# A four-block kernel: in the state-space stage the skip term goes to the matmul engine, the triangle to GpSimd, and one product changes its place; in the routing stage a subtraction is made in eight pieces

## The reference

```python
z, xBC, dt = split(x @ W_in)                       # 256, 384, 4 columns
xBC = silu(conv_b + sum(xp[:, k:k + L] * conv_w[:, k] for k in range(4)))
xh, B, C = split(xBC)                              # 4 heads of 64, 64, 64
dt = softplus(dt + dt_bias);  dA = dt * -exp(A_log);  A_cum = cumsum(dA)
Lmat = exp(where(tril, A_cum[l] - A_cum[s], -inf))  # the triangle
Y = einsum('ln,sn,hls,shp->lhp', C, B, Lmat, xh * dt)
Y = (Y + xh * D[:, None]) * silu(z)                # xh * D is the skip term
Y = Y * rsqrt(mean(Y * Y) + eps) * norm_w
out = Y @ W_out @ W_lin + b_lin
```

## Time and profile before

| | before |
|---|---|
| median of 3 runs | 1223.52 us (1223.49 to 1224.08) |
| the profiled execution: its own time | 1222.53 us |
| its span, first to last instruction | 1220.7 us |
| outside the span | 1.8 us |
| PE busy | 1028.3 us (84%) |
| DVE busy | 842.0 us (69%) |
| ACT busy | 712.4 us (58%) |
| POOL busy | 388.8 us (32%) |
| mean granted clock of PE | 0.901 |

### The profile page before, as it was taken

The page is one execution under the profiler, slowest core; times in us unless marked ns, Lnnn a source line. Parts: engine busy times, 40 slices in busy tenths (PEclk is TensorE's granted clock), DMA queues, the critical chain, the costliest instruction groups (busy, mean ns, idle before and its releaser), DMA issues. The chain is left out here.

```text
span 1220.7 us, 23165 instructions
## 1 busy us (share of the span) xinstructions
PE 1028.3 (84%) x6680; PEld 898.8 (74%) x6680; DVE 842.0 (69%) x2130; ACT 712.4 (58%) x1561; POOL 388.8 (32%) x421
## 2 busy tenths in 40 slices
PE   2999999999995857999998875567429999899997
PEld 2988988889884624666666664466419999799997
DVE  4577777877766468999999945799845555345554
ACT  4556565565662468889888825666315555355554
POOL 4223232232330000111111112556743444434445
PEclk9999999999998877888888777788559999899999
DMA  5121211211200023232223206534244444333331
GB/s 160 50 82 44 79 50 43 86 43 49 71 0 23 20 69 66 58 69 69 51 54 69 36 1 214 142 126 136 93 136 134 139 128 123 98 90 96 96 97 54
DMA packets 82344, 99.05 MB, mean 81 GB/s; under 512 B 9307, under 2 KB 68194, under 8 KB 82122
## 3 DMA queue, kind: packets, MB, share of 16 engines
q1 hardware_dynamic: 72058, 74.24, 22.5%
q0 software_dynamic: 8752, 21.25, 5.0%
q10 hardware_dynamic: 1440, 2.40, 0.6%
HBM read 72.23 MB, written 27.02 MB: 81 GB/s over the span
## 5 line engine op out<-in xcount | busy, mean ns | idle before, releaser
L1591 PE MATMUL e_p_y<-w,e_gT 128*128 (+1 forms) x852 | 118.2, 275 | 0.0
L1538 DVE TENSOR_TENSOR e_g<-e_sl,e_p_h 128x342 f32<-128x342 f32 x142 | 72.6, 511 | 64.2 <-ACT e_sl L1516 57.2
L1520 ACT ACTIVATE e_gT<-e_p_gx 128x384 f32<-128x384 f32 x142 | 69.8, 491 | 63.9 <-PE e_p_gx L1581 63.9
L1591 PEld LDWEIGHTS e_p_y<-w,e_gT 128*128 128x128 f32 (+1 forms) x852 | 106.1, 191 | 0.4 <-issue 0.4
L87 PE MATMUL e_p_h<-w_hi,e_xT_hi 128*128 x284 | 104.6, 368 | 1.8 <-issue 0.9
L1516 ACT ACTIVATE e_sl<-e_p_h 128x342 f32<-128x342 f32 x142 | 65.0, 458 | 69.9 <-PE e_p_h L89 69.9
L851 POOL TENSOR_TENSOR m_rs<-m_ms,m_minus_half 128x4 f32<-128x4 f32 x16 | 18.0, 1124 | 272.7 <-ACT m_ms L884 272.7
L1542 DVE TENSOR_TENSOR e_xT_lo<-e_p_gx,e_xT_hi 128x128 fp32r<-128x128 f32 x142 | 41.5, 292 | 86.0 <-ACT e_xT_hi L1524 85.6
L1502 POOL DMA_INDIRECT sorted_scratch<-e_xg x71 | 69.0, 972 | 90.7 <-DVE e_xg L1548 87.7
L1500 POOL DMA_INDIRECT out<-e_xg x71 | 68.8, 970 | 87.1 <-DVE e_xg L1548 79.7
L942 DVE SCALAR_TENSOR_TENSOR m_c<-m_p_x,m_vecs,m_c 128x506 f32<-128x506 f32 (+2 forms) x144 | 95.6, 740 | 0.0
(11 more groups left out here) (349 smaller groups left out, 3286.9 us busy)
## 6 DMA issues: line engine op xcount, KB each, us to landing
e_xg<-sorted_scratch SPq DMA_DIRECT2D x142, 130.0 KB, 2.1
m_cum<-cum_scratch SPq DMA_DIRECT2D x16, 1024.0 KB
g_adjT<-in_adjT SPq DMA_DIRECT2D x16, 512.0 KB, 3.8
g_adj<-in_adj SPq DMA_DIRECT2D x16, 512.0 KB, 4.7
c_adjT<-in_adjT SPq DMA_DIRECT2D x16, 512.0 KB, 6.4
x_tokens<-in_x SPq DMA_DIRECT2D x16, 256.0 KB, 4.9
sorted_scratch<-nothing SPq DMA_DIRECT2D x2, 1040.0 KB
sorted_scratch<-nothing SPq DMA_DIRECT2D x12, 130.0 KB, 1.9
```

Source lines behind the costliest of these rows:

```text
L1520: act.activation(gT[:, c % D3], p_gx[i % 2][:, 0:len(CH)], ACT.Copy).then_inc(q["gT_ready"], 1)
L1538: dve.tensor_tensor(g[:, i % D3], sl[:, i % 2], p_h3[i % 2][:, 0:HP], ALU.mult).then_inc(q["g_ready"], 1)
L1591: last = pe.matmul(p_y[d % 2][:, 0:P], gT[0:r, d % D3, k], w2k[:, bass.ts(e, P)], start=k == 0, stop=k == len(CH) - 1)
```

## The change

In the state-space stage the product of xh and D is made by PE: a diagonal matrix `skip` (eye times D, made once by DVE) is multiplied with xs into the same bank as Y, ahead of the two products of each head, so y1 and its two DVE instructions are gone, and y2 reads p_zY. The two triangle instructions go from DVE to POOL, in front of the two bias instructions. POOL's loop runs over iterations, and rs of step o = i - 4 stands behind triangle and bias of step s = i. Y of step v goes ahead of the product of C and B of step d on PE. Waits on y1 become waits on y2 or on Y. In the routing stage each of the two subtractions becomes eight, one for an expert.

```diff
         xdt = sb("xdt", [P, 2, T, DI])
-        y1 = sb("y1", [P, 2, S])
+        skip = sb("skip", [P, 2, P])
...
         @block.gpsimd
...
-            for s in range(STEPS):
-                for half in range(2):
-                    xt = X[:, s * T + 2 * half:s * T + 2 * half + 2, :]
-                    pool.tensor_tensor(xt, xt, bb, ALU.add).then_inc(q["biased"], 1)
-                need(pool, q["x_updated"], T * (s - 1))
-                pool.wait_ge(q["ms_ready"], s + 1)
-                pool.tensor_tensor(rs[:, s % 2], ms[:, s % 2], minus_half[:], ALU.pow).then_inc(q["rs_ready"], 1)
+            for i in range(END):
+                s, o = i, i - OUT
+                if live(s):
+                    pool.wait_ge(cum_in[s % 2], 16 * (s // 2 + 1))
+                    rows = cum[:, s % 2].rearrange("p h (g b l) -> p h g b l", g=G, b=2)
+                    for b in range(2):
+                        out = rows[:, :, :, b] if b == 0 else late[:, s % 2]
+                        pool.tensor_tensor(out, rows[:, :, :, b], never[:].rearrange("p (a b l) -> p a b l", a=1, b=1).broadcast_to([P, HEADS, G, P]), ALU.add).then_inc(q["masked"], 1)
+                    for half in range(2):
+                        xt = X[:, s * T + 2 * half:s * T + 2 * half + 2, :]
+                        pool.tensor_tensor(xt, xt, bb, ALU.add).then_inc(q["biased"], 1)
+                if live(o):
+                    need(pool, q["x_updated"], T * (o - 1))
+                    pool.wait_ge(q["ms_ready"], o + 1)
+                    pool.tensor_tensor(rs[:, o % 2], ms[:, o % 2], minus_half[:], ALU.pow).then_inc(q["rs_ready"], 1)
...
         @block.vector
         def _(dve):
+            for k in range(2):
+                dve.tensor_scalar(skip[:, k], eye[:], D[:, k:k + 1], None, ALU.mult).then_inc(q["skip_ready"], 1)
             for i in range(END):
                 s, d, v, y, o = i, i - DEC, i - W_LAG, i - GATED, i - OUT
                 if live(y):
                     dve.wait_ge(q["Y_done"], y + 1)
-                    dve.wait_ge(q["xs_ready"], y + 1)
-                    need(dve, q["y2_ready"], y)
-                    for k in range(2):
-                        dve.scalar_tensor_tensor(out=y1[:, k], in0=xs[:, y % 3, k], scalar=D[:, k:k + 1], in1=p_zY[:, k], op0=ALU.mult, op1=ALU.add).then_inc(q["y1_ready"], 1)
-                    dve.wait_ge(q["y1_ready"], 2 * (y + 1))
...
-                    dve.tensor_tensor(y2[:, y % 2], y1[:], zs[:, y % 3], ALU.mult).then_inc(q["y2_ready"], 1)
+                    dve.tensor_tensor(y2[:, y % 2], p_zY[:], zs[:, y % 3], ALU.mult).then_inc(q["y2_ready"], 1)
...
-                if live(s):
-                    dve.wait_ge(cum_in[s % 2], 16 * (s // 2 + 1))
-                    rows = cum[:, s % 2].rearrange("p h (g b l) -> p h g b l", g=G, b=2)
-                    for b in range(2):
-                        out = rows[:, :, :, b] if b == 0 else late[:, s % 2]
-                        dve.tensor_tensor(out, rows[:, :, :, b], never[:].rearrange("p (a b l) -> p a b l", a=1, b=1).broadcast_to([P, HEADS, G, P]), ALU.add).then_inc(q["masked"], 1)
...
         @block.tensor
...
+                if live(v):
+                    pe.wait_ge(q["zs_ready"], min(s + 1, STEPS))
+                    need(pe, q["y2_ready"], v)
+                    if live(o):
+                        pe.wait_ge(q["ms_ready"], o + 1)
+                    pe.wait_ge(q["W_ready"], 2 * (v + 1))
+                    pe.wait_ge(q["xdt_ready"], v + 1)
+                    pe.wait_ge(q["xs_ready"], v + 1)
+                    pe.wait_ge(q["skip_ready"], 2)
+                    for g in range(G):
+                        for h in range(HEADS):
...
+                            pe.matmul(p_zY[p0:p0 + HD, k, l0:l0 + N], skip[:, k, p0:p0 + HD], xs[:, v % 3, k, l0:l0 + N], start=True, stop=False)
+                            pe.matmul(p_zY[p0:p0 + HD, k, l0:l0 + N], xdt[:, v % 2, 2 * g, hs], W[:, v % 2, g, h, 0:N], start=False, stop=False)
+                            last = pe.matmul(p_zY[p0:p0 + HD, k, l0 + P:l0 + N], xdt[:, v % 2, 2 * g + 1, hs], W[:, v % 2, g, h, N:NB], start=False, stop=True)
+                    last.then_inc(q["Y_done"], 1)
                 if live(d):
                     pe.wait_ge(q["xdt_ready"], d + 1)
...
                     last.then_inc(q["G_done"], 1)
-                if live(v):
...
-                            pe.matmul(p_zY[p0:p0 + HD, k, l0:l0 + N], xdt[:, v % 2, 2 * g, hs], W[:, v % 2, g, h, 0:N], start=True, stop=False)
-                            last = pe.matmul(p_zY[p0:p0 + HD, k, l0 + P:l0 + N], xdt[:, v % 2, 2 * g + 1, hs], W[:, v % 2, g, h, N:NB], start=False, stop=True)
-                    last.then_inc(q["Y_done"], 1)
...
                     dst = weights[n][1]
                     pool.wait_ge(q["w_hi"], 4 + n + 1)
-                    pool.tensor_tensor(dst.lo[:, :, 0:H], raw[n], dst.hi[:, :, 0:H].bitcast(F32), ALU.subtract).then_inc(q["w_split"], 1)
+                    for e in range(EX):
+                        pool.tensor_tensor(dst.lo[:, e, 0:H], raw[n][:, e], dst.hi[:, e, 0:H].bitcast(F32), ALU.subtract).then_inc(q["w_split"], 1)
...
-            pool.wait_ge(q["w_split"], 2)
+            pool.wait_ge(q["w_split"], 2 * EX)
```

More of the change, by code:

```diff
@@ L822, in mamba_phase @@
         names = ("consts w2_done w2_ready x_done first_tap taps z_done zs_ready xs_ready B_ready C_ready xh_done xdt_ready G_done "
[L823 removed]
+                 "masked dec_ready W_ready Y_done y2_ready sq_ready ss_done ms_ready rs_ready out_done biased x_updated skip_ready")
         q = {s: sem(s) for s in names.split()}
@@ L864, in _ @@
                     act.wait_ge(q["taps"], 9 * (d + 1))
-                    need(act, q["y1_ready"], 2 * (d - 2))
+                    need(act, q["Y_done"], d - 2)
                     need(act, q["xh_done"], d - 2)
@@ L967, in _ @@
                     need(pe, q["zs_ready"], s)
-                    need(pe, q["y1_ready"], 2 * (s - 2))
+                    need(pe, q["y2_ready"], s - 2)
                     for k in range(2):
@@ L979, in _ @@
                     pe.wait_ge(q["zs_ready"], min(s + 1, STEPS))
-                    need(pe, q["y1_ready"], 2 * min(s - 2, STEPS))
+                    need(pe, q["y2_ready"], min(s - 2, STEPS))
                     pe.wait_ge(q["sq_ready"], o + 1)
@@ L1001, in _ @@
                     last.then_inc(q["G_done"], 1)
-                if live(v):
-                    pe.wait_ge(q["zs_ready"], min(s + 1, STEPS))
-                    need(pe, q["y1_ready"], 2 * (v - 0))
-                    if live(o):
-                        pe.wait_ge(q["ms_ready"], o + 1)
-                    pe.wait_ge(q["W_ready"], 2 * (v + 1))
-                    pe.wait_ge(q["xdt_ready"], v + 1)
-                    for g in range(G):
-                        for h in range(HEADS):
-                            k, p0 = h // 2, h % 2 * HD
-                            hs = slice(h * HD, (h + 1) * HD)
-                            l0 = g * N
-                            pe.matmul(p_zY[p0:p0 + HD, k, l0:l0 + N], xdt[:, v % 2, 2 * g, hs], W[:, v % 2, g, h, 0:N], start=True, stop=False)
-                            last = pe.matmul(p_zY[p0:p0 + HD, k, l0 + P:l0 + N], xdt[:, v % 2, 2 * g + 1, hs], W[:, v % 2, g, h, N:NB], start=False, stop=True)
-                    last.then_inc(q["Y_done"], 1)
 BF16 = mybir.dt.bfloat16
```

4 lines of the change are left out of this document (3 added, 1 removed).

## The result

The changed kernel takes 1203.42 us (median of 4 runs, 1202.8 to 1205.4); before, beside it on the same chip, took 1223.51. The profiled execution has a span of 1201.0 us and a mean granted clock of 0.927 (before 0.901).

What follows compares the result with a forecast made beforehand. The prediction took a 16.80 us loop through ACT to bound the state-space stage's middle, with DVE deciding at its start. Terms -9.1 - 1.6 - 0.4 + 2.2 = -8.9 gave 1214.6 us, range 1205 to 1221.

Steps and rivals of the forecast that it cites:

- Start: State-space stage up to zs of step 4: without the triangle on DVE, taps start earlier; -9.1 us.
- Rival (D): Start of the state-space stage: PE at half clock makes z late, half of the 9.1 goes; 1219 us, chance 0.10.
- Middle: 11 iterations of the state-space stage, zs of step 4 to step 15: half of a 3.2 us bound, -1.6 us.
- The loop through ACT: State-space stage: table load, zs, ms, exponentials, sq take 16.80 us an iteration; the change does not touch it.
- Rival (B): Middle of the state-space stage: PE becomes the bound if its clock stays at 0.80; +7.8 us, 1224.0, chance 0.10.
- Drain: State-space stage behind the last projection: y1 and xdt wait saved, skip products added; -2.1 to +1.3, taken as -0.4 us.
- the wait for xdt: Drain term: PE's wait for xdt lies on the path once and goes; 1.3 us saved.
- POOL's triangle: State-space stage: 2.35 us an instruction on POOL, costing nothing up to about 4.8 us each.
- (C): Rival in the state-space stage: POOL is late with the triangle, 6 us an instruction; 1230 us, chance 0.06.
- Routing: Routing stage's split subtractions: DVE held until the eighth piece ends, 1.1 us more, twice; +2.2 us.
- Rival (A): Routing stage: DVE does get in between the pieces, saving 1.4 to 8.6 us; 1203.8 to 1211.0, chance 0.19.
- lower branch: Low case of Rival (A): four chained DVE instructions behind the first each meet a new piece; saves only 1.4 us.

Runs made afterwards that it cites:

- only_tri: The kernel before with one edit, the triangle moved from DVE to POOL; 1227.73 us, ratio 0.9941 to before on the same chip.
- fill_skip: no_skip with PE also making the eight skip products, from a matrix of zeros that adds nothing; 1209.07 us, ratio 0.9864 to before.
- no_skip: The changed kernel with the skip term back on DVE (y1, two instructions); 1230.88 us, ratio 0.9968 to before on the same chip.
- bias4: The changed kernel with the routing stage's bias as four plain 128 x 128 instructions in place of one broadcast; ratio 0.9827 to before.

## Why the prediction was right or wrong

**Start: right, by its own steps.** Taps end at 429.70 + 5.53 = 435.23 (said 435.9), zs of step 4 at 483.73 (said 484.3). only_tri keeps 8.6 of it by itself. Rival (D) did not come.

**Middle: the size right, the reason half.** The loop through ACT holds it (16.80, then 16.98). But what DVE loses, 1.41 and 2.28 an iteration, gave nothing in the middle: with the order and the products there, y1 back on DVE makes the middle 185.60, and the triangle back 185.68, against 185.81. The skip products, which I had priced as a cost with room for it, are what the gain rests on: they stand where PE would wait for the taps. Rival (B), at 0.10, is real without the order edit and absent with it: PE's clock went from 0.85 to 0.95 over the middle.

**Drain: the failed step.** "Behind the last projection y1 lies on the path three times, 4.2, and the wait for xdt once, 1.3" and two Y with products "2 x 1.7 to 2 x 3.4", together between -2.1 and +1.3. The term that was mis-sized is the wait for xdt, 1.3, which was all that I gave the order of Y and C B. Measured, from the runs' drains: y1 away -3.77 (fill_skip 53.62 to after 49.85; said -4.2); the products +6.24 (no_skip 47.38 to fill_skip 53.62; said 3.4 to 6.8); the order **-8.37** (only_tri 55.75 to no_skip 47.38; between -5.5 and -9.3 in the four pairs), which stood in my sum as -1.3. I had counted only the idle time that PE shows ahead of C B. Gone with it are xdt and C B themselves, 4.18 with the wait, and low clock behind waits: PE waits 1.12 us ahead of the last Y in no_skip and this Y takes 2.8 us; in only_tri it waits 2.63 and takes 4.3, before 2.63 and 5.4. The last sums of squares take 1.84 in no_skip and 3.41 in only_tri. With the 0.89 by which only_tri differs from before, the four make the -6.79 of the table. The sum goes through one trace of each kernel; with the drain of 51.0 that six others with the changed stage have, y1 gives 2.6 and the whole drain 5.6, so the order stays the term that failed.

**POOL's triangle: right.** 2.35 us, as the slope of the earlier trace rows gave, and nothing waits for it; (C) did not come.

**Routing: the wrong sign.** "DVE to be held until the eighth piece ends", +2.2; it was let in behind each piece, and the two steps concerned are 1.3 us shorter together. Of this the whole stage keeps 0.2 to 0.3. Rival (A) was right in its lower branch (1.4), to which I gave too little. The Trainium skill (SBUF — State Buffer, Who interferes with whom) says that of two instructions which need the ports that DVE and POOL share, the first to issue has them for the whole instruction and the other is blocked; it does not say who is next when POOL has another instruction ready. The chain was let in after the first, 0.84 for a piece of 0.91. The denominators were not: L1347 at 794.39, after, was held for 1.85 us, past the end of the bias that ran when it issued and to the end of the next. In the traces of all 18 kernels I counted the two-operand instructions on DVE's small tiles that met a POOL instruction with another close behind: some 160 ended with the first, some 25 were passed over (a few depend on where the line is drawn), 18 of these being the denominators (18 of 21 of them). Neither the form of POOL's instruction (bias4), nor the time left until the next (0.1 to 1.3 us where passed over, 0.1 to 0.9 where not), nor the DVE instruction alone (the difference of the logits three times each way) decides it. **What decides stays open**; my row of before was one of those passed over, and I made a rule of it.

What is left of the 19.7 us of the profiled executions, 0.6 ahead of the state-space stage and 0.8 in the experts, no edit touches; I did not follow it up.

## What to carry to other kernels

When instructions are reordered, price the whole distance that leaves the path (what runs between the two ends), not the idle time that the trace shows there. Edits to a closed pipeline don't add: order and skip term cost 13 and 24 us alone and gave 2 together, so test a combination before an edit is thrown away. And where PE waits once an iteration ahead of long matmuls that lie in a loop, as here for 2.90 us, look whether work can be moved into that gap: here the clock behind the gap was worth 15 us, the relief of DVE nothing in the middle and 3.8 in the drain, and the products cost 6.2 in the drain.
